# New tables for the order of work in a CIN and top-MLP kernel

## The chip, the cores and the metric

The kernel runs on one core of one Trainium2 chip. The metric is the device time of one execution in microseconds, as the median of the runs shown; lower is better.

## The reference, cut to what matters

Everything is float32. 512 samples each have 32 categorical fields; every field has a table of 16-wide rows. Three interaction layers and a small MLP follow:

```python
e = jnp.stack([tbl_f[ids[:, f]] for f in range(32)], axis=1)        # (512, 32, 16)
x0 = xk = e
for W in (W0, W1, W2):             # (32, 32, 64), (32, 64, 64), (32, 64, 64)
    xk = relu(jnp.einsum('bmd,bhd,mhk->bkd', x0, xk, W))             # (512, 64, 16)
    outs.append(jnp.sum(xk, axis=2))                                 # (512, 64)
h = jnp.concatenate([*outs, dense_ctx], axis=1)                      # (512, 208)
h = jnp.maximum(h @ W_top1 + b_top1, 0)                              # 512 wide
h = jnp.maximum(h @ W_top2 + b_top2, 0)                              # 256 wide
y = h @ W_top3                                                       # (512, 1)
```

## The kernel before

**Tiles and blocks.** The batch is cut into 8 pairs of 64 samples; a sample has 16 columns, so a pair has 1024. The first two pairs are cut in half again, which gives ten blocks (`BLOCKS`): blocks 0 to 3 are narrow (512 columns), 4 to 9 wide (1024). A *step* (layer, block) is one interaction layer of one block. Steps of layers 1 and 2 multiply 16 tiles of 128 rows (eight tiles of four fields, by two halves `g` of 32 of the 64 hidden rows) elementwise by a factor, and contract each product with weights on TensorE into 64 output rows. A layer-0 step has four tiles and a quarter-size one, the "opposite" product, because it uses the symmetry of the two equal operands.

**Who does what.** GpSimd gathers the table rows, one indirect DMA of 128 rows for each of 128 gathers (16 for a pair, 8 for a narrow block), with `gather` at L692 to L721. SyncE's queue copies a block's rows to DRAM (`scratch`) and loads them back, repeated over partitions, as `own`, `opposite` and `rotated` (`layer0_operands`, for layer 0) and as eight field tiles (`field_tiles`, for layers 1 and 2), in the order of `LOADS`. SyncE's queue is in order: a load that waits holds all that stand behind it. VectorE makes most products (L805, and L840, L845 in the narrow layer-0 steps) into a ring `vz` of nine tiles; GpSimd makes the rest (L746 into the four-tile ring `pz`; L729 for the opposite product into `oz`). `POOL_TILES` says how many of a step's 16 tiles GpSimd makes. TensorE contracts them (L1060), ScalarE takes the relu (L934), VectorE sums over the 16 columns of a sample (L855). The narrow blocks' layer-0 factors come from the gathered rows by matmuls ("turns", L998).

**The factor of layers 1 and 2** is the relu's output, each row repeated four times. Three ways lead to it. For a step in no table, ScalarE sends DMAs from the relu's output to `hidden` (the relay, L945) and copies `hidden` into PSUM (L890). For a step in `SPREAD`, TensorE writes both halves into PSUM by matmuls with a 0/1 matrix (L984), with no relay, and ScalarE copies one half to `hidden` (L904) if GpSimd has tiles of that step. For a step in `HALF`, TensorE writes the first half alone and the second goes by relay.

**Paired steps.** In a narrow step each weight meets 512 columns, usually in two matmuls of 256, one for each half of the output. For a step in `PAIRED` one matmul of 512 columns takes a tile, even tiles into the lower 64 rows and odd ones into the upper (L1055). At its end ScalarE copies the accumulator (`fold`, L917), TensorE adds the two halves with a 0/1 matrix (`join`, L1082), and the relu waits for that. The join stands in TensorE's order one item behind the step's last product.

**The order.** Nothing is decided at run time. `BEGUN` lists the 30 steps; VectorE's, TensorE's, GpSimd's and ScalarE's programs are derived from it (`vector_program`, `tensor_program`, `POOLS`, `scalar_program`), and each engine runs its own in order, with semaphores between them. `tensor_program` puts a spread behind the product that `spread_after` gives: soon after its source step has ended, or once the factor's place (a ring of three) is free. A step's products on TensorE stand as VectorE's and GpSimd's interleaved. `FIRST_GATHERS` gathers go ahead of GpSimd's first product; `GATHERS_IN` says how many go directly ahead of each product of a step. `PACED` lets gather `i` wait until TensorE has used so many of VectorE's products; `BEHIND_SPREAD` lets it wait for so many spreads. Block b's scratch waits for all its gathers (L586, L596 in `scratch`).

## Time and profile before

| what | value |
|---|---|
| runs shown | 338.79, 339.94, 414.93 us |
| median | 339.94 us |
| span of the profiled execution | 356.2 us |
| TensorE matmul busy | 314.8 us (88%) |
| VectorE busy | 282.1 us (79%) |
| GpSimd busy | 246.0 us (69%) |
| ScalarE busy | 53.3 us (15%) |

The page gives no other time of the profiled execution than its span, from its first to its last instruction. Busy times don't count DMA issues, semaphores or branches. The ends of matmuls are modelled, so back-to-back matmuls are better read from the chain of waits, which goes from start to start. All engines' times are microseconds from the start of the span, and a gather on GpSimd is a row of L719.

### The profile page before, as it was taken

The page shows a single profiled execution, that of the slowest core. Times are in us where ns is not written, and L with a number is a line of the kernel's source. Part 1 is how long each engine was busy: PE and PEld are TensorE (multiplying, and loading weights), DVE is VectorE, ACT ScalarE, POOL GpSimd, SP SyncE. Part 2 cuts the span into 40 slices and gives each one's busy share as a digit, 9 for nine tenths or more (in the row PEclk, how much of TensorE's full clock was granted, in tenths as well). Part 3 has the DMA queues.
Part 4 walks back from the last instruction along what each step waited for, and adds up shares of the span by engine and source line. Part 5 has one row for each costly group of instructions (what it writes and reads, how often), then busy time and mean ns, then how long its engine had stood idle before and what let it go on. Part 6 is the DMA issues. An engine that isn't in the chain of part 4 may idle for free.

```text
span 356.2 us, 4290 instructions
## 1 busy us (share of the span) xinstructions
PE 314.8 (88%) x1602; PEld 114.9 (32%) x1602; DVE 282.1 (79%) x172; ACT 53.3 (15%) x77; POOL 246.0 (69%) x195
## 2 busy tenths in 40 slices
PE   0378588988699788898999999998999999999997
PEld 0344224432222223332333333332333333333334
DVE  0039477869499878999999999999998879999220
ACT  1000011012020221110112120121022111220011
POOL 5646566766367668869997987896998569729300
PEclk9999989999899999999999999999999999999999
DMA  6272853834875982979499989683699897050000
GB/s 183 65 231 72 230 154 73 230 71 110 295 240 174 326 292 65 326 217 280 167 317 289 296 284 297 201 268 67 215 346 337 290 291 194 17 133 2 0 0 0
DMA packets 34302, 68.09 MB, mean 191 GB/s; under 512 B 5866, under 2 KB 15082, under 8 KB 34282
## 3 DMA queue, kind: packets, MB, share of 16 engines
q1 hardware_dynamic: 23562, 56.80, 49.0%
q10 hardware_dynamic: 6624, 9.96, 9.4%
q0 software_dynamic: 4096, 1.06, 3.5%
q8 instruction: 12, 0.20, 0.2%
q14 instruction: 8, 0.07, 0.1%
HBM read 55.55 MB, written 2.03 MB: 162 GB/s over the span
## 4 chain that ended last, share of the span: by engine, by line
PE 59%; POOL 16%; issue 11%; DVE 9%; another core or an unknown queue 2%; DMA 1%; DVEq 1%; ACT 0%; POOLq 0%; SPq 0%
PE acc L1060 37%; PE acc L1055 12%; POOL gathered L719 10%; DVE vz L805 8%; POOL pz L746 6%; PE factor L984 2%; PE factor L1093 2%; PE factor L1021 1%; PE factor L1088 1%; PE acc L1050 1%; PE factor L998 1%; PE acc L1082 1%; PE factor L1100 1%; DVEq L800 1%
## 5 line engine op out<-in xcount | busy, mean ns | idle before, releaser
L805 DVE TENSOR_TENSOR vz<-fields_sb,factor 128x1024 f32<-128x1024 f32 (+3 forms) x113 | 230.5, 2090 | 20.7 <-PE factor L984 7.6
L1060 PE MATMUL acc<-vz,w_sb 128*64 128x512 f32 (+1 forms) x800 | 172.6, 569 | 10.9 <-DVE vz L805 3.6
L719 POOL DMA_INDIRECT gathered<-in_table,index x128 | 121.6, 950 | 65.0 <-issue 31.5
L746 POOL TENSOR_TENSOR pz<-fields_sb,hidden 128x1024 f32<-128x1024 f32 (+1 forms) x52 | 117.9, 2292 | 19.4 <-DMA hidden<-relu_out 9.6
L1060 PEld LDWEIGHTS acc<-vz,w_sb 128*64 128x64 f32 x800 | 57.8, 139 | 113.7 <-issue 98.6
L1055 PE MATMUL acc<-vz,w_sb 128*64 128x512 f32 x216 | 60.9, 621 | 3.7 <-DVE vz L805 2.9
L1060 PE MATMUL acc<-pz,w_sb 128*64 128x512 f32 x192 | 48.1, 594 | 0.3 <-POOL pz L746 0.3
L934 ACT ACTIVATE relu_out<-acc 128x512 f32<-128x512 f32 (+1 forms) x30 | 15.3, 512 | 126.3 <-PE acc L1060 47.3
L890 ACT ACTIVATE factor<-hidden 128x1024 f32<-128x1024 f32 (+1 forms) x23 | 20.1, 878 | 65.8 <-DMA hidden<-relu_out 34.3
L805 DVE TENSOR_TENSOR vz<-rotated,factor 128x2048 f32<-128x2048 f32 x12 | 26.9, 2279 | 1.8 <-issue 1.8
L1055 PEld LDWEIGHTS acc<-vz,w_sb 128*64 128x64 f32 x216 | 16.4, 139 | 36.4 <-issue 24.6
L855 DVE TENSOR_REDUCE feats<-relu_out 128x32 f32<-128x512 f32 (+1 forms) x30 | 17.1, 571 | 7.9 <-ACT relu_out L934 7.7
L1060 PEld LDWEIGHTS acc<-pz,w_sb 128*64 128x64 f32 x192 | 13.5, 137 | 28.1 <-issue 23.9
L1021 PE MATMUL factor<-gathered,unit_sb 32*128 32x128 f32 x8 | 1.6, 493 | 15.0 <-DMA gathered<-in_table,index 15.0
L984 PE MATMUL factor<-relu_out,unit_sb 32*128 32x512 f32 (+1 forms) x68 | 11.4, 553 | 3.8 <-issue 3.3
L917 ACT ACTIVATE folds<-acc 128x512 f32<-128x512 f32 x7 | 4.2, 597 | 47.5 <-PE acc L1055 43.4
L845 DVE TENSOR_TENSOR vz<-own,factor 128x1024 f32<-128x1024 f32 x4 | 4.7, 1217 | 6.4 <-remote 4.1
L1050 PE MATMUL acc<-oz,w0c_sb 128*64 128x256 f32 (+1 forms) x72 | 8.3, 349 | 1.3 <-POOL oz L729 1.3
L822 DVE TENSOR_TENSOR vz<-own,factor 128x512 f32<-128x512 f32 x2 | 1.4, 688 | 9.8 <-ACT own L896 9.3
L890 ACT ACTIVATE factor<-own 128x1024 f32<-128x1024 f32 x6 | 6.2, 1026 | 13.0 <-POOL pz L746 13.0
L984 PEld LDWEIGHTS factor<-relu_out,unit_sb 32*128 32x128 f32 x68 | 3.9, 190 | 12.7 <-issue 11.8
L774 DVE TENSOR_TENSOR w_sb<-vz 128x256 f32<-128x256 f32 x1 | 0.4, 425 | 8.5 <-DMA w0c_sb<-in_w0c 8.5
(44 smaller groups left out, 83.2 us busy)
## 6 DMA issues: line engine op xcount, KB each, us to landing
fields_sb<-fields SPq DMA_DIRECT2D x48, 512.0 KB
rotated<-fields SPq DMA_DIRECT2D x24, 512.0 KB
fields_sb<-fields SPq DMA_DIRECT2D x32, 256.0 KB
hidden<-relu_out ACTq DMA_DIRECT2D x30, 256.0 KB, 5.6
own<-fields SPq DMA_DIRECT2D x6, 512.0 KB
gathered<-in_table,index POOLq DMA_INDIRECT x128
hidden<-relu_out ACTq DMA_DIRECT2D x16, 128.0 KB
fields<-gathered SPq DMA_DIRECT2D x6, 256.0 KB, 5.2
```

Of the source, the lines that this page charges most:

```text
L719: nc.gpsimd.indirect_dma_start(gathered[:, pair % GRING, j, :], None, table, bass.IndirectOffsetOnAxis(ap=index[:, i:i + 1], axis=0)).then ...
L746: nc.gpsimd.tensor_tensor(pz[:, at % PRING, 0:cols], fields[s][:, t, col:col + cols], hidden_of(step, g), ALU.mult).then_inc(pz_ready, 1)
L805: nc.vector.tensor_tensor(vz[:, at:at + nt, 0:cols].rearrange("p t (a n) -> p t a n", n=half), src[:, t:t + nt, col:col + cols].rearrange( ...
L855: nc.vector.tensor_reduce(feats[layer][:, pair, first:first + count], relu_of(step).rearrange("p (b d) -> p b d", d=DIM), op=ALU.add, axis ...
L890: nc.scalar.activation(factor_of(step, g), src.rearrange("p (a n) -> p a n", a=2), ACT.Copy).then_inc(factor_put, 1)
L934: nc.scalar.activation(relu_of(step), acc[:, n % 2, 0:half], ACT.Relu).then_inc(relu_done, 1)
L984: last = nc.tensor.matmul(factor_of(step, g)[:, ab, :], unit_sb[row:row + HROWS, :], relu_of(before)[row:row + HROWS, :], start=True, stop ...
L1021: last = nc.tensor.matmul(slot_of(step, held)[:, ab, wave * quarter:(wave + 1) * quarter], by, rows[row, :], start=True, stop=True)
L1050: last = nc.tensor.matmul(acc_of(step, q // 2)[:, part], w0c_sb[:, by_field(b), q, :], quarters, start=False, stop=q % 2 == 1)
L1055: last = nc.tensor.matmul(acc[side % 2 * HID:(side % 2 + 1) * HID, ORDER.index(step) % 2, 0:cols], w_sb[layer][:, kt, :], z, start=side < ...
L1060: last = nc.tensor.matmul(acc_of(step, ab), w_sb[layer][:, kt, :], z[:, ab * half:(ab + 1) * half], start=start and j == 0, stop=stop and ...
L1093: return nc.tensor.matmul(to, wt2_sb[:, k, m * P:(m + 1) * P], rows, start=k == 0, stop=k == F_TOP1 // P - 1)
```

## The change

Only tables at the head of the file are set anew; no function changes.

- `BEGUN`: (1,3) goes ahead of (2,2); (2,3) ahead of (0,5), which then stands between (2,3) and (1,4); (0,6) ahead of (2,4); (2,6) ahead of (0,8).
- `SPREAD` and `HALF`: (1,4) and (1,5) turn from whole spreads to halves; (2,2) and (1,3) from halves to whole ones; (2,4), (1,7) (halves) and (1,9) (whole) leave the tables and go by relay.
- `POOL_TILES`: GpSimd's tiles in the narrow steps go from 4 to 7, in the wide ones from 48 to 46.
- `FIRST_GATHERS`, `GATHERS_IN`, `PACED`, `BEHIND_SPREAD`: 23 gathers ahead of the first product for 21; the rows of gathers between products are cut otherwise (the longest 21 for 24), the waits are other ones, and many of them ask for fewer products.
- `PAIRED`: (1,2) alone is left of seven.
- `LOADS`: block 1's field tiles go behind block 2's operands; block 3's field tiles ahead of block 4's scratch and operands.

```diff
-BEGUN = [(0, 0), (1, 0), (0, 1), (2, 0), (0, 2), (1, 1), (0, 3), (1, 2), (2, 1), (2, 2), (1, 3), (0, 4), (0, 5),
-    (2, 3), (1, 4), (1, 5), (2, 4), (0, 6), (2, 5), (0, 7), (1, 6), (1, 7), (0, 8), (2, 6), (2, 7), (0, 9), (1,
-    8), (1, 9), (2, 8), (2, 9)]
+BEGUN = [(0, 0), (1, 0), (0, 1), (2, 0), (0, 2), (1, 1), (0, 3), (1, 2), (2, 1), (1, 3), (2, 2), (0, 4), (2,
+    3), (0, 5), (1, 4), (1, 5), (0, 6), (2, 4), (2, 5), (0, 7), (1, 6), (1, 7), (2, 6), (0, 8), (2, 7), (0,
+    9), (1, 8), (1, 9), (2, 8), (2, 9)]
...
-SPREAD = [(1, 0), (2, 3), (1, 4), (1, 5), (1, 9)]
-HALF = [(2, 0), (1, 2), (2, 2), (1, 3), (2, 4), (1, 7), (2, 7)]
-POOL_TILES = {(1, 0): 0, (2, 0): 0, (1, 1): 1, (2, 1): 0, (1, 2): 0, (2, 2): 0, (1, 3): 0, (2, 3): 3, (1, 4): 1,
-    (1, 5): 5, (2, 4): 3, (2, 5): 4, (1, 6): 4, (1, 7): 3, (2, 6): 4, (2, 7): 5, (1, 8): 6, (1, 9): 4, (2, 8): 3,
-    (2, 9): 6}
-FIRST_GATHERS = 21
-GATHERS_IN = {(0, 1): (2,), (0, 2): (11,), (1, 1): (1,), (0, 3): (7,), (0, 4): (24,), (0, 5): (15,), (2, 3): (2,
-    0, 1), (1, 4): (2,), (1, 5): (10, 0, 0, 2, 0), (2, 4): (3, 0, 0), (0, 6): (2,), (2, 5): (7, 0, 0, 0), (1, 6):
-    (0, 1, 0, 2), (1, 7): (3, 4, 0), (0, 8): (8,)}
-PACED = {12: 1, 13: 2, 14: 4, 17: 5, 18: 6, 19: 7, 20: 8, 22: 9, 24: 11, 25: 14, 26: 15, 28: 16, 29: 17, 30: 18,
...
-    74, 97: 78, 99: 80, 102: 83, 104: 84, 106: 85, 107: 86, 109: 87, 112: 96, 114: 97, 117: 99, 119: 100, 121:
-    102, 122: 103, 125: 104, 126: 105, 127: 106}
-BEHIND_SPREAD = {10: 1, 11: 3, 15: 4, 24: 5, 26: 6, 36: 7, 43: 8, 45: 9, 55: 10, 61: 11, 80: 12, 85: 13, 93: 14}
+SPREAD = [(1, 0), (1, 3), (2, 2), (2, 3)]
+HALF = [(2, 0), (1, 2), (1, 4), (1, 5), (2, 7)]
+POOL_TILES = {(1, 0): 0, (2, 0): 0, (1, 1): 2, (2, 1): 1, (1, 2): 1, (2, 2): 0, (1, 3): 0, (2, 3): 3, (1, 4):
+    0, (1, 5): 4, (2, 4): 3, (2, 5): 4, (1, 6): 4, (1, 7): 3, (2, 6): 5, (2, 7): 5, (1, 8): 5, (1, 9): 4, (2,
+    8): 5, (2, 9): 4}
+FIRST_GATHERS = 23
+GATHERS_IN = {(0, 2): (10,), (1, 1): (1, 3), (1, 2): (3,), (2, 1): (10,), (0, 4): (3,), (2, 3): (21, 2, 2),
+    (0, 5): (5,), (1, 5): (8, 4, 0, 2), (2, 4): (0, 3, 1), (2, 5): (1, 9, 0, 0), (1, 6): (1, 0, 2, 0), (1, 7):
+    (6, 2, 1), (2, 6): (2, 0, 0, 1, 1), (0, 8): (1,)}
+PACED = {12: 1, 13: 2, 14: 3, 15: 4, 16: 4, 18: 4, 20: 7, 21: 8, 22: 10, 24: 11, 25: 13, 26: 14, 27: 15, 28:
...
+    78, 103: 78, 104: 79, 105: 79, 106: 80, 109: 81, 111: 88, 112: 92, 114: 93, 115: 93, 116: 93, 117: 93,
+    119: 94, 122: 98, 126: 101, 127: 102}
+BEHIND_SPREAD = {10: 1, 24: 5, 36: 7, 45: 9, 48: 9, 50: 9, 61: 11, 80: 12, 84: 12, 85: 13, 91: 13, 100: 14,
+    104: 14, 105: 14, 107: 14, 117: 14, 122: 14}
...
-PAIRED = [(2, 0), (1, 1), (1, 2), (2, 1), (2, 2), (1, 3), (2, 3)]
+PAIRED = [(1, 2)]
...
-LOADS = [('scratch', 0), ('fields', 0), ('scratch', 1), ('operands', 1), ('fields', 1), ('scratch', 2),
-    ('operands', 2), ('scratch', 3), ('operands', 3), ('fields', 2), ('scratch', 4), ('operands', 4), ('fields',
-    3), ('scratch', 5), ('operands', 5), ('fields', 4), ('fields', 5), ('scratch', 6), ('operands', 6),
+LOADS = [('scratch', 0), ('fields', 0), ('scratch', 1), ('operands', 1), ('scratch', 2), ('operands', 2),
+    ('fields', 1), ('scratch', 3), ('operands', 3), ('fields', 2), ('fields', 3), ('scratch', 4), ('operands',
+    4), ('scratch', 5), ('operands', 5), ('fields', 4), ('fields', 5), ('scratch', 6), ('operands', 6),
...
```

The rest of `LOADS` is the same in both: scratch and operands of a block, then field tiles, up to `('scratch', 9), ('operands', 9), ('fields', 8), ('fields', 9)`.

## Rows read from the trace of the kernel before

**Rows 1.** The page's head.

```profile
span 356.2 us, 4290 instructions
```

**Rows 2.** Busy time by stretch: engines' busy us (instructions), granted clock, DMA share, GB/s.

```profile
75.00:100.00 25.00, 20.69 (x99) 7.22 (x99) 20.14 (x19) 4.06 (x8) 15.09 (x16) 0.93 0.64 192
250.00:300.00 50.00, 50.00 (x242) 16.82 (x240) 45.84 (x22) 8.02 (x10) 42.12 (x20) 1.00 0.87 283
```

**Rows 3.** VectorE in order of time: start, us, what [idle before <- its releaser].

```profile
41.56 2.48 DVE L840 TENSOR_TENSOR vz<-own,factor 128x512 f32<-128x512 f32 x4 [3.47 <-remote]
97.43 1.75 DVE L805 TENSOR_TENSOR vz<-fields_sb,factor 128x1536 f32<-128x1536 f32 x1 [4.86 <-PE acc L1055]
126.94 2.29 DVE L805 TENSOR_TENSOR vz<-rotated,factor 128x2048 f32<-128x2048 f32 x1 [1.84 <-issue]
141.79 3.35 DVE L805 TENSOR_TENSOR vz<-fields_sb,factor 128x3072 f32<-128x3072 f32 x1 [1.26 <-issue]
277.44 3.35 DVE L805 TENSOR_TENSOR vz<-fields_sb,factor 128x3072 f32<-128x3072 f32 x1 [2.33 <-PE acc L1060]
291.47 6.62 DVE L805 TENSOR_TENSOR vz<-fields_sb,factor 128x3072 f32<-128x3072 f32 x2 [1.83 <-issue]
```

**Rows 4.** TensorE in order of time, the spread for (2,2).

```profile
92.46 0.70 PE L984 MATMUL factor<-relu_out,unit_sb 32*128 32x256 f32 x4 [3.29 <-issue]
```

**Rows 5.** The chain of waits in order of time: start, us, what.

```profile
60.17 1.08 PE acc L1060 x8
...
76.44 1.73 PE acc L1060 x16
...
88.74 0.43 PE acc L1082 x4
...
165.45 1.06 PE factor L984 x4
...
290.28 1.07 PE factor L984 x8
291.35 46.50 PE acc L1060 x216
```

**Rows 6.** ScalarE in order of time: three relus, and copies of a factor.

```profile
92.02 0.38 ACT L934 ACTIVATE relu_out<-acc 128x256 f32<-128x256 f32 x1 [3.62 <-issue]
...
103.52 0.38 ACT L934 ACTIVATE relu_out<-acc 128x256 f32<-128x256 f32 x1 [0.36 <-PE acc L1082]
...
125.55 0.38 ACT L934 ACTIVATE relu_out<-acc 128x256 f32<-128x256 f32 x1 [2.83 <-PE acc L1082]
125.83 1.02 ACT L890 ACTIVATE factor<-own 128x1024 f32<-128x1024 f32 x1
...
239.47 1.03 ACT L890 ACTIVATE factor<-hidden 128x1024 f32<-128x1024 f32 x1 [3.81 <-DMA hidden<-relu_out]
```

**Rows 7.** Groups by shape: count, busy us, mean ns of one, idle time before them.

```profile
L746 POOL TENSOR_TENSOR pz<-fields_sb,hidden 128x1024 f32<-128x1024 f32 x48 | 112.8, 2375 | 19.3 <-DMA hidden<-relu_out 9.6 <-PE acc L1060 5.1 <-DMA fields_sb<-fields 2.0
L805 DVE TENSOR_TENSOR vz<-fields_sb,factor 128x3072 f32<-128x3072 f32 x30 | 99.6, 3345 | 5.4 <-issue 3.1 <-PE acc L1060 2.3
L805 DVE TENSOR_TENSOR vz<-fields_sb,factor 128x1024 f32<-128x1024 f32 x43 | 49.9, 1212 | 8.7 <-PE factor L984 7.6 <-remote 1.1
L805 DVE TENSOR_TENSOR vz<-fields_sb,factor 128x1536 f32<-128x1536 f32 x14 | 24.3, 1748 | 6.6 <-PE acc L1055 6.3 <-PE acc L1060 0.3
```

**Rows 8.** GpSimd in order of time, from (1,5)'s fourth product to gather 127.

```profile
168.82 4.72 POOL L746 TENSOR_TENSOR pz<-fields_sb,hidden 128x1024 f32<-128x1024 f32 x2
...
174.98 0.94 POOL L719 DMA_INDIRECT gathered<-in_table,index  x1 [0.30 <-issue]
...
247.10 0.94 POOL L719 DMA_INDIRECT gathered<-in_table,index  x1 [1.70 <-PE acc L1060]
248.06 0.73 POOL L729 TENSOR_TENSOR oz<-gathered,opposite 128x256 f32<-128x256 f32 x1
```

**Rows 9.** SyncE's queue: the field tiles of blocks 8 and 9.

```profile
258.19 29.40 SPq L653 DMA_DIRECT2D fields_sb<-fields  x16
```

More of the change, by code:

```diff
@@ L118 @@
 IN_FLIGHT_DIRECT = 3
-LOADS = [('scratch', 0), ('fields', 0), ('scratch', 1), ('operands', 1), ('fields', 1), ('scratch', 2),
-    ('operands', 2), ('scratch', 3), ('operands', 3), ('fields', 2), ('scratch', 4), ('operands', 4), ('fields',
-    3), ('scratch', 5), ('operands', 5), ('fields', 4), ('fields', 5), ('scratch', 6), ('operands', 6),
-    ('scratch', 7), ('operands', 7), ('fields', 6), ('fields', 7), ('scratch', 8), ('operands', 8), ('scratch',
-    9), ('operands', 9), ('fields', 8), ('fields', 9)]
+LOADS = [('scratch', 0), ('fields', 0), ('scratch', 1), ('operands', 1), ('scratch', 2), ('operands', 2),
+    ('fields', 1), ('scratch', 3), ('operands', 3), ('fields', 2), ('fields', 3), ('scratch', 4), ('operands',
+    4), ('scratch', 5), ('operands', 5), ('fields', 4), ('fields', 5), ('scratch', 6), ('operands', 6),
+    ('scratch', 7), ('operands', 7), ('fields', 6), ('fields', 7), ('scratch', 8), ('operands', 8),
+    ('scratch', 9), ('operands', 9), ('fields', 8), ('fields', 9)]
 OWN, ACROSS = -1, L0TILES
```

7 rows, old and new, of the table PACED are left out of this document.

## The prediction

> **What bounds the kernel now.** I read the page's span, then busy time by stretch, the idle time in front of VectorE's products, the chain of waits, and the queues of ScalarE, GpSimd and SyncE. The profiled execution's span is 356.2 us [rows 1]; the page gives no other time for it. The median of the three runs shown is 339.94 us, 16.3 us less than this span, so the profiled execution was slow. I work the sum in its microseconds, take it off the median too, and say which stalls may belong to the profiled execution alone.
>
> There are two regimes. From 250 to 300 us TensorE is busy 50.00 of 50 us; from 75 to 100 it is busy 20.69 of 25 and VectorE 20.14 [rows 2]. Late, VectorE waits for TensorE: 2.33 us at 277.4 (no free slot in `vz`) and 1.83 us at 291.5 [rows 3]. In the chain the last stage of it is 216 matmuls in 46.50 us with no gap, 215 ns each, and behind them come the top layers [rows 5]. So late the end moves with TensorE's work. Early it moves with VectorE's stalls, because TensorE is fed by it.
>
> **The change part by part**, by step (layer, block).
>
> (a) *Block 5's layer 0 goes behind (2,3).* Its second product, at 126.94, came after 1.84 us of idling [rows 3]. The profile shows why in ScalarE's queue: the relu of (1,3) ran at 125.55, having waited 2.83 us for the join of that paired step, and block 5's factor copy stood behind it [rows 6]. After the change (1,3) has no join, and 13 tiles of (2,3) lie ahead of (0,5). I take -1.84. The step (1,4) started after 1.26 us of waiting for its spread at 141.79 [rows 3]; now (0,5), two products of 2.3 us, stands between, long enough to cover that: -1.26. What is late next is the matmul queue itself.
>
> (b) *One join for seven.* A join costs TensorE 0.43 us [rows 5]; six go, 2.6 us, all before 150 us, where TensorE is not the limit. I count them at nothing; TensorE's idle quarter to eighth there is the cover, and if it is gone the gain is 2.6. The unpaired step issues 64 matmuls of 256 columns for 32 of 512. Sixteen of 256 took 1.73 us, 108 ns each [rows 5], half of 215, so the width costs nothing by this row. The bigger stall is at 92.46: TensorE stood 3.29 us in front of the spread for (2,2), which waited for the relu of the paired (1,2) [rows 4], and VectorE then lost 4.86 us at 97.43 for want of a slot [rows 3]. In the new order that spread stands behind (1,3)'s fourth product, far from the relu. The gain lies between 0 and 4.86. That relu came 3.62 us after ScalarE's previous work, while the relu of the next paired step idled 0.36 us [rows 6], with the same code. I therefore hold most of this stall for the profiled execution's own and take -0.5, nearest to the ordinary join.
>
> (c) *Loads.* Block 1's field tiles now follow block 2's operands on SyncE's queue, so block 1's `own` copy flies alone. VectorE waited 3.47 us for (0,1) at 41.56 [rows 3], released by something the profile cannot name. Bounds: -3.47, or a little above 0 if the later tiles hold (1,1). I take 0, since (2,0) behind it needs the relu of (1,0) in any case. Block 3's tiles go ahead of block 4's operands, which (1,3)'s earlier place needs; block 4's step is not due until some 30 us later, which hides it.
>
> (d) *GpSimd tiles.* VectorE gives three narrow tiles away, 1748 - 1212 = 536 ns each, 1.6 us, and takes back two wide ones, 3345 / 3 = 1115 ns each, 2.2 us [rows 7]. Net +0.6, with ends -1.6 (the wide ones hidden in VectorE's 4.2 us of late waiting for TensorE) and +2.2. The early products stand ahead of gathers on GpSimd; the gathers' weaker waits pay for them.
>
> (e) *Other spreads.* A spread of a wide step holds TensorE 1.06 us as a half (four matmuls) and 1.07 as a whole (eight) [rows 5], so turning (1,4) and (1,5) into halves gives nothing; three wide ones disappear, those of (2,4), (1,7) and (1,9): 3 x 1.07 = -3.2 us in TensorE's saturated stretch. In their place ScalarE sends DMAs and copies 1.03 us per factor [rows 6], with 10 us or more of other steps as cover; if that is gone, up to 3.2 is given back. The narrow ones only change kind.
>
> (f) *(2,6) ahead of (0,8), and where the gathers stand.* (2,6) now starts where (0,8) did, at about 239.4, but its factor is copied from 239.47 to 240.50 [rows 6]: +1.1. The last gather, 127, now stands behind all five products of (2,6). From the start of (1,5)'s fourth product GpSimd had 30 gathers and 16 large products up to the end of gather 127, 168.82 to 248.04, 79.2 us [rows 8]; now it has 31 gathers and 20 large products from there: 31 x 1.25 + 20 x 2.375 [rows 7] + 2 small ones x 0.74 = 87.7 (1.25 from the 0.95 of a gather and the 0.30 in front of it [rows 8]). It comes 8.5 us later if GpSimd is as late there as now. Behind it on SyncE are block 9's scratch, its operands, and then the field tiles of block 8, from 258.19, 29.40 us for 16 [rows 9]: 1.84 us each, so the eighth is in by about 258.2 + 8 x 1.84 + 3 x 1.84 = 278.4 (an estimate, three in flight). (1,8)'s second product needs it at 277.44 + 3.35 + 0.5 = 281.3 [rows 3]. So 2.9 of the 8.5 are slack and VectorE may wait 5.6. The cover is VectorE's 2.33 + 1.83 us of waiting for TensorE, and that GpSimd comes earlier, since its gathers' waits for matmuls loosen (1.70 us in front of gather 127 alone [rows 8]). I take 0 for the tiles, with 5.6 as the other end.
>
> Sum: -1.84 - 1.26 - 0.5 + 0.6 - 3.2 + 1.1 = -5.1 us. That makes 351.1 of the profiled 356.2, and **334.8** of the median 339.94.
>
> A rule speaks against (b). The Trainium skill's page "TensorE: Matmul & The Clock Gate", section "Back-to-back issue gap", says that in a stream of weight loads and matmuls the spacing is set by both, 81 ns at 128 columns and 131 ns at 512. Read between these, two matmuls of 256 would take about 196 ns against 131 (an estimate from that page), and 192 such pairs 12.5 us more, which would turn the sum into +7.4. The 108 ns against 215 of this kernel's rows disagree with it.
>
> **The rivals.** A measurement of this kernel can tell about 2%, 6.8 us: faster is below 333.1, slower above 346.7.
>
> 1. *The early stalls belong to every run.* Then the 4.86 us at 97.43 go whole: 334.8 - 4.4 = 330.4, and 327.8 if the six joins also counted. For it: the stall hangs on an order in which a spread stands straight behind a join, and that order goes. Against it: the relu's lateness has no cause in the rows, and the median is 16.3 us under the span.
>
> 2. *GpSimd's last gather becomes the path.* Block 9's rows come late, block 8's tiles behind them on SyncE's queue later still, and (1,8) waits. Early gains are then waited out, since GpSimd's own chain sets the time: 339.94 + 5.6 + 1.1 - 1.07 (the spread behind it) = 345.6, slower than before. It decides from the point where gather 127 is issued over 2.9 us later than 247.1, counted against (1,7)'s end. For it: the count of 87.7 against 79.2. Against it: VectorE's 4.2 us of slack and the looser waits.
>
> 3. *The gain doesn't reach the end.* The three engines are so evenly loaded late that without the spreads TensorE waits for VectorE, which has 2.2 us more to do there, and (a)'s stalls turn up in front of (1,4) in another form: 339.94 - 3.2 + 2.2 = 338.9.
>
> 4. *Narrow matmuls are dearer.* Eight of 256 columns alone span 1.08 us in the chain [rows 5], 135 ns each with their drain. At that price 384 cost 51.8 us against 192 x 0.215 = 41.3: +10.5 on TensorE early, and with no cover 334.8 + 10.5 = 345.3. The row of 16 speaks against it, and only pieces of the stretch could pay it. The page named above is what would favour it.
>
> **How the numbers follow.** Chances: forecast 0.45, rival 1 0.22, rival 2 0.17, rival 3 0.11, rival 4 0.05. The forecast's own range is 331 to 338.5. The whole range reaches down to 328 (rival 1 with the joins) and up to 343, which takes in rival 3 and the lower part of rivals 2 and 4. Faster by over 2%: a third of the forecast and nearly all of rival 1, 0.37. Slower by over 2%: a third of rival 2 and of rival 4, 0.08. Within 2%: 0.55.
>
> **What would show it.** In the changed profile the products of (0,5) and (1,4) should start with no wait; no spread should follow a join with TensorE standing; TensorE should have no gap from about 165 us on, with one wide spread left there beside that of (1,5). VectorE should wait for TensorE, not for field tiles, in front of (1,8). If it waits there for tiles, and gather 127 was issued later than some 10 us behind the end of (1,7)'s products, rival 2 is right. If TensorE shows holes behind GpSimd's products of (2,5) or (2,6), part (f) was priced too low. If the early stretch still loses 3 to 4 us at a time with no order behind it, those stalls are not the tables' doing.

## The result and the profile after

The changed kernel takes **360.17 us** (median of 5 runs, 359.79 to 364.84) against 339.73 of the kernel before, run beside it: a ratio of 1.064, 95% interval [1.061, 1.068]. It is slower by 20.4 us, where 334.8 was forecast and the range ended at 343. Medians here and below are over all runs, while ratios are worked out from the single runs without the disturbed ones (414.93 us of the kernel before, one run each of e4 and e13), so that a ratio is not the quotient of two medians.

The page of the changed kernel, its head, its first part and its chain of waits by engine, and below that the chain of the kernel before, from its second profile (run e5 below):

```profile
span 363.0 us, 4599 instructions
## 1 busy us (share of the span) xinstructions
PE 311.2 (86%) x1754; PEld 124.5 (34%) x1754; DVE 283.0 (78%) x171; ACT 51.8 (14%) x72; POOL 245.9 (68%) x196
...
PE 40%; DMA 26%; DVE 15%; issue 9%; POOL 6%; SPq 2%; ACT 1%; ACTq 0%; DVEq 0%; POOLq 0%
```

```profile
PE 78%; DVE 12%; issue 5%; POOL 2%; DMA 1%; DVEq 0%; ACT 0%; SPq 0%
```

No engine has over 1 us more to do than in the table of the time before. What has grown is the waiting: DMA is 26% of the chain that ended last, for 1%.

Both profiled spans must first be put side by side with care. The kernel before was profiled once more (run e5 below): 339.09 us with a span of 337.3, not 356.2 [rows 1]. This clean profile is what the changed kernel is held against from here on. The changed kernel's own profiled execution took 364.84 us, 4.7 above its median: its rows show where it waits and for what, and the price of a wait is read from the runs further down. Its file is two lines longer, so that a gather is a row of L721. Busy time by stretch of the changed kernel (columns as in [rows 2]), then of the clean kernel before:

```profile
75.00:100.00 25.00, 24.30 (x170) 11.62 (x170) 25.00 (x25) 1.97 (x4) 18.19 (x19) 0.93 0.59 184
150.00:200.00 50.00, 40.63 (x184) 13.39 (x186) 47.22 (x22) 10.39 (x12) 40.54 (x31) 0.99 0.83 268
275.00:300.00 25.00, 17.60 (x72) 5.70 (x70) 16.30 (x7) 3.27 (x5) 12.31 (x6) 0.86 0.93 309
```

```profile
75.00:100.00 25.00, 24.24 (x108) 7.73 (x106) 24.44 (x23) 4.89 (x9) 18.00 (x20) 1.00 0.73 228
150.00:200.00 50.00, 50.00 (x244) 17.14 (x240) 49.86 (x23) 10.19 (x12) 44.12 (x30) 1.00 0.85 277
250.00:300.00 50.00, 50.00 (x242) 16.80 (x240) 47.31 (x22) 8.98 (x11) 32.68 (x16) 1.00 0.71 219
```

In the clean kernel before, TensorE is busy 50.00 of 50 us from 150 to 200 and VectorE 49.86: both are full. After the change TensorE has holes there (40.63 of 50) and a large one from 275 to 300.

The holes are named by the idle time in front of TensorE's matmuls. TensorE of the changed kernel in order of time (start, us, what [idle before <- releaser]):

```profile
118.62 0.65 PE L1062 MATMUL acc<-pz,w_sb 128*64 128x256 f32 x4 [1.51 <-POOL pz L748]
122.31 0.65 PE L1062 MATMUL acc<-pz,w_sb 128*64 128x256 f32 x4 [2.17 <-POOL pz L748]
...
190.93 2.77 PE L1062 MATMUL acc<-vz,w_sb 128*64 128x512 f32 x12
198.64 1.61 PE L1062 MATMUL acc<-pz,w_sb 128*64 128x512 f32 x4 [4.93 <-POOL pz L748]
...
281.40 4.26 PE L1062 MATMUL acc<-vz,w_sb 128*64 128x512 f32 x12 [2.85 <-DVE vz L807]
...
291.06 4.49 PE L1062 MATMUL acc<-vz,w_sb 128*64 128x512 f32 x12 [4.55 <-DVE vz L807]
```

The three with a `pz` wait for GpSimd's products of (2,3) and (2,5), the last two for VectorE in (1,8). VectorE there, in order of time:

```profile
277.90 3.35 DVE L807 TENSOR_TENSOR vz<-fields_sb,factor 128x3072 f32<-128x3072 f32 x1 [3.70 <-DMA fields_sb<-fields]
...
287.65 3.35 DVE L807 TENSOR_TENSOR vz<-fields_sb,factor 128x3072 f32<-128x3072 f32 x1 [5.81 <-ACT factor L892]
...
302.71 3.35 DVE L807 TENSOR_TENSOR vz<-fields_sb,factor 128x3072 f32<-128x3072 f32 x1 [2.38 <-DMA fields_sb<-fields]
```

The same place in the clean kernel before, the first products of (1,8) and (1,9):

```profile
258.55 3.35 DVE L805 TENSOR_TENSOR vz<-fields_sb,factor 128x3072 f32<-128x3072 f32 x1 [0.86 <-PE acc L1060]
...
272.57 6.62 DVE L805 TENSOR_TENSOR vz<-fields_sb,factor 128x3072 f32<-128x3072 f32 x2 [1.83 <-issue]
```

These answer to the last two of [rows 3]: where VectorE waited 0.86 us for TensorE it now waits 3.70 for a field tile. The 5.81 are put down to a factor copy, but (1,8)'s own two copies had run at 270.16 and 274.08, and the one that ended at 287.60 is (1,9)'s. What that product still needed was a field tile: it multiplies tiles 3 to 5, and GpSimd's third product of (1,8), which takes tile 5 alone, waited for its tile up to 287.60 too (below). So all three are waits for tiles. GpSimd of the changed kernel in order of time, and then SyncE's queue, show where the tiles were:

```profile
62.63 0.46 POOL L731 TENSOR_TENSOR oz<-gathered,opposite 128x128 f32<-128x128 f32 x1 [4.91 <-DMA opposite<-fields]
...
70.01 1.27 POOL L748 TENSOR_TENSOR pz<-fields_sb,hidden 128x512 f32<-128x512 f32 x1 [3.29 <-DMA fields_sb<-fields]
...
195.24 0.95 POOL L721 DMA_INDIRECT gathered<-in_table,index  x1 [0.30 <-issue]
196.21 6.98 POOL L748 TENSOR_TENSOR pz<-fields_sb,hidden 128x1024 f32<-128x1024 f32 x3
...
252.62 0.98 POOL L721 DMA_INDIRECT gathered<-in_table,index  x1 [0.16 <-issue]
...
280.09 2.35 POOL L748 TENSOR_TENSOR pz<-fields_sb,hidden 128x1024 f32<-128x1024 f32 x1 [12.98 <-DMA fields_sb<-fields]
...
287.60 7.00 POOL L748 TENSOR_TENSOR pz<-fields_sb,hidden 128x1024 f32<-128x1024 f32 x3 [2.16 <-DMA fields_sb<-fields]
```

```profile
45.80 8.85 SPq L655 DMA_DIRECT2D fields_sb<-fields  x8
...
106.23 0.38 SPq L593 DMA_DIRECT2D fields<-gathered  x1
...
254.95 0.38 SPq L593 DMA_DIRECT2D fields<-gathered  x1
...
264.08 33.25 SPq L655 DMA_DIRECT2D fields_sb<-fields  x16
```

The last gather, 127, is issued at 252.62; block 9's scratch follows at 254.95 and the field tiles of blocks 8 and 9 from 264.08, in 33.25 us for 16 where [rows 9] had 29.40 from 258.19. GpSimd itself idles 12.98 us for such a tile. The three products at 196.21 are those of (2,5) that TensorE waited for at 198.64; nine gathers stood ahead of them. In the clean kernel before gather 127 was issued at 228.19, 24.4 us sooner. Part of that is its place and part a lag of everything in front: VectorE's last product of (1,7) ended at 222.0 there and at 237.5 here, so that behind that product gather 127 came after 6.2 us and comes after 15.1, 8.9 us more.

GpSimd of the clean kernel before, in the stretch where this lag begins, and its SyncE queue:

```profile
63.73 0.47 POOL L729 TENSOR_TENSOR oz<-gathered,opposite 128x128 f32<-128x128 f32 x1
...
66.90 0.94 POOL L719 DMA_INDIRECT gathered<-in_table,index  x1 [0.30 <-issue]
68.14 0.94 POOL L719 DMA_INDIRECT gathered<-in_table,index  x1 [0.30 <-issue]
...
130.15 0.94 POOL L719 DMA_INDIRECT gathered<-in_table,index  x1 [0.30 <-issue]
131.40 0.94 POOL L719 DMA_INDIRECT gathered<-in_table,index  x1 [0.30 <-PE acc L1060]
```

```profile
32.59 9.73 SPq L653 DMA_DIRECT2D fields_sb<-fields  x8
...
96.02 0.38 SPq L591 DMA_DIRECT2D fields<-gathered  x1
```

A gather is busy for 0.94 us and the next one starts 1.25 us after it, with 0.30 us "issue" between. From gather 43 at 65.65 to gather 80 at 114.12 there are 37 in 48.5 us, 1.31 us each with one opposite product among them, and waits beyond the 0.30 come to under 2 us in all: GpSimd has practically no slack in this stretch, although the windows count it busy 18.00 of 25 us. What is put in front of these gathers, a product or a wait, can be made up only out of those 2 us. Here block 1's field tiles were issued from 32.59, ahead of the loads of blocks 2 and 3; in the changed kernel they were issued from 45.80, ahead of block 3's loads and block 2's tiles, and the two waits of GpSimd at 62.63 and 70.01 are for block 3's `opposite` and a tile of block 2. VectorE of the changed kernel waits for tiles of blocks 1 and 2 as well, in (1,1) and (1,2):

```profile
58.28 2.35 DVE L807 TENSOR_TENSOR vz<-fields_sb,factor 128x1024 f32<-128x1024 f32 x2 [2.86 <-DMA fields_sb<-fields]
...
73.81 2.35 DVE L807 TENSOR_TENSOR vz<-fields_sb,factor 128x1024 f32<-128x1024 f32 x2 [2.93 <-DMA fields_sb<-fields]
```

In the changed kernel gather 47 was issued 9.6 us later than in the clean one (80.22 for 70.64), gather 63 12.0 later (103.81 for 91.83), and block 5's scratch, which waits for gather 63, 10.2 later (106.23 for 96.02).

### The profile page after: what moved, and what is told of

Read it like the earlier page. It is cut to its first block, busy times and chain, and to the rows that moved or that the text cites. A ratio compares the mean times of both kernels' runs of the same rounds, so it can differ in the third digit from the quotient of the medians.

```text
span 363.0 us, 4599 instructions
## 1 busy us (share of the span) xinstructions
PE 311.2 (86%) x1754; PEld 124.5 (34%) x1754; DVE 283.0 (78%) x171; ACT 51.8 (14%) x72; POOL 245.9 (68%) x196
## 4 chain that ended last, share of the span: by engine, by line
PE 40%; DMA 26%; DVE 15%; issue 9%; POOL 6%; SPq 2%; ACT 1%; ACTq 0%; DVEq 0%; POOLq 0%
PE acc L1062 33%; DVE vz L807 14%; DMA fields_sb<-fields 12%; DMA fields<-gathered 5%; POOL gathered L721 4%; DMA hidden<-relu_out 4%; DMA rotated<-fields 4%; PE acc L1057 2%; POOL pz L748 2%; PE factor L1095 2%; DMA gathered<-in_table,index 1%; PE factor L1090 1%; SPq L655 1%; PE acc L1052 1%; PE factor L1102 1%
## 5 line engine op out<-in xcount | busy, mean ns | idle before, releaser
L1062 PE MATMUL acc<-vz,w_sb 128*64 128x512 f32 (+1 forms) x1168 | 225.3, 521 | 18.8 <-DVE vz L807 17.1
L721 POOL DMA_INDIRECT gathered<-in_table,index x128 | 122.3, 955 | 39.6 <-issue 27.1
L1062 PEld LDWEIGHTS acc<-vz,w_sb 128*64 128x64 f32 x1168 | 83.3, 140 | 145.8 <-issue 93.2
L1062 PE MATMUL acc<-pz,w_sb 128*64 128x512 f32 (+1 forms) x208 | 51.2, 582 | 12.3 <-POOL pz L748 12.2
L892 ACT ACTIVATE factor<-hidden 128x1024 f32<-128x1024 f32 (+1 forms) x27 | 25.2, 932 | 95.8 <-DVE vz L807 44.6
L1062 PEld LDWEIGHTS acc<-pz,w_sb 128*64 128x64 f32 x208 | 14.7, 138 | 42.6 <-issue 22.0
L1057 PE MATMUL acc<-vz,w_sb 128*64 128x512 f32 x30 | 9.3, 714 | 2.1 <-DVE vz L807 2.0
L731 POOL TENSOR_TENSOR oz<-gathered,opposite 128x256 f32<-128x256 f32 (+1 forms) x9 | 5.8, 645 | 6.7 <-DMA opposite<-fields 6.7
L986 PE MATMUL factor<-relu_out,unit_sb 32*128 32x256 f32 (+1 forms) x52 | 7.6, 476 | 0.5 <-ACT relu_out L936 0.5
L1052 PEld LDWEIGHTS acc<-oz,w0c_sb 128*64 128x64 f32 x72 | 4.8, 137 | 5.9 <-issue 2.9
L871 DVE TENSOR_SCALAR vz<-factor,bt_sb 128x512 f32<-128x512 f32 x2 | 1.5, 751 | 6.6 <-PE factor L1102 6.6
## 6 DMA issues: line engine op xcount, KB each, us to landing
hidden<-relu_out ACTq DMA_DIRECT2D x12, 128.0 KB, 4.2
```

The costliest lines, as they stand in the source:

```text
L721: nc.gpsimd.indirect_dma_start(gathered[:, pair % GRING, j, :], None, table, bass.IndirectOffsetOnAxis(ap=index[:, i:i + 1], axis=0)).then ...
L731: nc.gpsimd.tensor_tensor(oz[:, 0:quarter], quarter_rows(step[1]), opposite[s][:, at:at + quarter], ALU.mult).then_inc(pz_ready, 1)
L892: nc.scalar.activation(factor_of(step, g), src.rearrange("p (a n) -> p a n", a=2), ACT.Copy).then_inc(factor_put, 1)
L986: last = nc.tensor.matmul(factor_of(step, g)[:, ab, :], unit_sb[row:row + HROWS, :], relu_of(before)[row:row + HROWS, :], start=True, stop ...
L1052: last = nc.tensor.matmul(acc_of(step, q // 2)[:, part], w0c_sb[:, by_field(b), q, :], quarters, start=False, stop=q % 2 == 1)
L1057: last = nc.tensor.matmul(acc[side % 2 * HID:(side % 2 + 1) * HID, ORDER.index(step) % 2, 0:cols], w_sb[layer][:, kt, :], z, start=side < ...
```

## The experiments

Theory **G** is that GpSimd's order is the cause: rows of gathers ahead of products that TensorE needs, and products and waits ahead of gathers that the loads need. Rival **P** is that the stalls seen before belong to the profiled execution; **L1** that SyncE's new order of loads costs by itself; **N** (the prediction's rival 4) that narrow matmuls are dearer. Differences below are between medians; where two kernels ran on different chips, the ratio to the kernel before is given beside.

**e1 to e4: the rows of gathers of the changed kernel, cut otherwise.**

```
e1:  (2, 6): (2, 0, 0, 1, 1), (0, 8): (1,)   ->  (2, 6): (5, 0, 0, 0, 0)
e2:  (2, 5): (1, 9, 0, 0)                    ->  (2, 5): (10, 0, 0, 0)
e3:  (2, 3): (21, 2, 2), (0, 5): (5,)        ->  (2, 3): (17, 0, 0), (0, 5): (13,)
e4:  all three
```

> The changed kernel with gathers 123 to 127 all ahead of (2,6)'s first GpSimd product, nothing else. Theory G (gather rows stand in the wrong places): block 9's rows come some 12 us sooner, block 8's field tiles start when (2,6) is done, the waits in front of (1,8) (3.70, 5.81 and 2.38 us on VectorE, 2.85 and 4.55 on TensorE) go, and the time falls by 5 to 8 us, to 352 to 355. Rival L (load order and narrow matmuls make the loss early, and the late waits are only where it surfaces): the waits move elsewhere and the time stays within 2 us of 360.2.

> The changed kernel with the nine gathers ahead of (2,5)'s second GpSimd product moved ahead of its first. Theory G: TensorE's wait of 4.93 us for that product at 198.6, and the half clock behind it, mostly go, while the first product comes some 2 us late: 3 to 6 us less, 354 to 357. Rival L: within 2 us of 360.2, because the wait for block 8's tiles further on sets the time whatever happens here.

> The changed kernel with 17 gathers ahead of (2,3)'s first GpSimd product instead of 21 and none between its three products; the eight go ahead of (0,5)'s. Theory G: TensorE's three waits for these products (1.51, 2.17, 1.12 us) go and block 3's end comes 4 us sooner; 2 to 5 us less, 355 to 358. Rival L: within 2 us of 360.2.

> The three edits of the gather rows together. Theory G: the sum of them less what overlaps, 10 to 17 us less, 343 to 350, with the rest of the loss left for load order or narrow matmuls. Rival L: under 6 us less.

e1: 353.63 us, 6.5 less than 360.17 (ratio to the kernel before 1.042 [1.038, 1.046]), as theory G has it; gather 127 is issued at 237.25, and of VectorE's waits for tiles in (1,8) and (1,9) none is left, while the one in front of (2,7) grew from 1.64 to 3.80. e2 and e3 gained nothing: 362.73 (1.065 [1.060, 1.070]) and 362.34 (1.067 [1.062, 1.071]); both expectations missed. Together (e4) they gave 348.98 (1.026 [1.023, 1.030]), 11.2 less. So e2's and e3's cuts are worth nothing while gather 127 stays where it was (253.24 and 250.34 in them): (1,8) waits the gain out again (3.52 and 5.10 us in e2, 3.52 and 5.49 in e3), as the prediction's rival 2 has it. With gather 127 in its new place they are worth 4.65 (e4 against e1). In e3 the wait for (2,3)'s products turned into one for the opposite product of (0,5). In e4 it is still there; TensorE in order of time:

```profile
130.36 1.97 PE L1052 MATMUL acc<-oz,w0c_sb 128*64 128x256 f32 x8 [5.94 <-POOL oz L731]
```

**e5: the kernel before, profiled again.**

> The kernel before, unchanged, profiled once more. Theory P (the profiled execution of before was slow by itself): span near 338 us, and the stalls of 4.86 us at 97.4 and 3.47 us at 41.6 on VectorE are gone or under 1 us, so that the step (1,5) ends some 15 us sooner than at 171.8. Rival: span near 356 again with the same stalls, which then belong to the tables.

339.09 us, span 337.3. The stalls of 4.86 us at 97.43 and of 3.29 on TensorE at 92.46 [rows 3, 4] are gone, as is the 1.26 in front of (1,4); the 3.47 at 41.56 is 1.17. The one in front of (0,5) is there (1.75 us); it is the first of that step's two products, not the second as the prediction has it. P holds: most of the early stalls of the first profile were that execution's own, as the prediction guessed.

**e6: other rows once more, for the whole kernel.** Against e4, the gathers of (0,5) go into (1,5), and those of (2,4) to (2,6) are cut otherwise.

```
(1, 5): (25, 4, 0, 0), (2, 4): (0, 2, 1), (2, 5): (4, 0, 0, 0), (1, 6): (2, 2, 2, 0), (1, 7): (6, 2, 2), (2, 6): (6, 0, 0, 0, 0)
```

> The mended gather rows of the last run, and besides no gathers ahead of (0,5)'s product (they go to (1,5), where GpSimd waits for field tiles), and those of (2,5) spread further on. Theory G: TensorE's wait of 5.9 us for that product and VectorE's 3.1 us in (2,5) go, 3 to 6 us less than 349.0: 343 to 346, within 2% of before. Rival L: what is left of the loss is early, in load order or narrow matmuls, and the time stays at 347 to 350.

A miss: 352.70 (1.037 [1.031, 1.043]), 3.7 more than e4. The waits moved, to 4.8 us in front of (2,7) and 2.1 in (0,6). A row of gathers can't be placed by hand for one waiting product at a time.

**e7 and e8, from e6: the loads, and the pairing.**

```
e7:  LOADS: ('operands', 1), ('fields', 1), ('scratch', 2), ...     (block 1's field tiles as before)
e8:  PAIRED = the seven steps of the kernel before
```

> As e6, with block 1's field tiles behind block 1's operands again, as before. Theory L1 (late tiles of block 1 hold (1,1), and push block 2's tiles and (1,2) back): VectorE's waits for field tiles at 56 and 71 us (1.6 and 3.4) go, 2 to 5 us less than e6. Rival: own copy of block 1 then flies beside them, (0,1) waits instead, and nothing is gained.

> As e6, with all seven narrow steps paired again. Theory G says that unpairing cost nothing: within 2 us of e6, or up to 3 us slower, since six joins and folds come back. Rival N (narrow matmuls are dearer than their row showed, or the added instructions have to be fetched): 4 to 10 us faster than e6.

e7: 348.25 (1.024 [1.019, 1.029]), 4.45 less than e6, as L1 has it. VectorE's waits for tiles in (1,1) and (1,2) are gone (2.72 and 3.94 us in e6), and GpSimd's two (5.25 and 2.92 in e6) are nothing and 0.44; gather 47 comes at 74.31 for 80.98. Which of the two engines' waits carries the 4.45 isn't told apart. e8: 351.40 (1.036 [1.032, 1.040]), not told apart from e6. N fails: with the tables of this order the unpaired steps cost nothing that could be measured.

**e9, from e7: the early GpSimd products back as before.**

```
POOL_TILES (1, 1): 2 -> 1, (2, 1): 1 -> 0, (1, 2): 1 -> 0, with the gathers around them cut as (1, 1): (1,), (0, 3): (6,), (0, 4): (13,)
```

> The kernel of e7 with the early GpSimd products as before: (1,1) gives 1 tile to GpSimd, (1,2) and (2,1) none, and gathers 24 to 63 are cut as before around them. Theory E: an early GpSimd product that waits for a field tile or a relay holds the gathers of pairs 2 and 3 that stand behind it in GpSimd's order; so gather 63 comes some 7 us sooner than at 100 us in e7, block 4's field tiles and block 6's operands are loaded sooner, the waits in (1,4) (4.7 us together) and (0,6) (3.6) go in part, and the time is 3 to 6 us below e7's 348.25: 342 to 345. Rival: gather 63 is set by its own waits and the loads ahead of it in SyncE's queue; VectorE only takes three narrow tiles more (3 x 0.54 = 1.6 us), and the time is 347 to 350.

345.99 (1.019 [1.016, 1.022]), 2.3 less than e7, between theory and rival, and the intervals overlap. Gather 63 came 2.7 us sooner (96.37 for 99.09), not 7. VectorE makes one product more in (1,1) than in e7, and the waits of `PACED` count its products and were left as they were, so that behind it each asks for one product fewer: part of the 2.3 may be that.

**e10 to e12, and e14 to e16: one part of the change alone, in the kernel before.**

```
e10: PAIRED = [(1, 2)]
e11: (2, 4), (1, 7) out of HALF, (1, 9) out of SPREAD
e12: POOL_TILES (1, 1): 2, (2, 1): 1, (1, 2): 1; gathers (1, 1): (1, 0), (0, 3): (7,), (1, 2): (3,), (2, 1): (10,), (0, 4): (11,)
e14: block 1's field tiles behind block 2's operands
e15: (2, 3) ahead of (0, 5); gathers (2, 3): (12, 0, 1), (0, 5): (5,)
e16: (2, 6) ahead of (0, 8); gathers (2, 6): (8, 0, 0, 0)
```

> The kernel before with one change alone: of seven paired steps only (1,2) stays paired. The prediction's term (b): six joins of 0.43 us go where TensorE is not the limit; time unchanged to 2.6 us less (337 to 339.7, against 339.7). Rival 4 (narrow matmuls are dearer): up to 10.5 us more, 342 to 350.

> The kernel before with one change alone: the spreads of (2,4), (1,7) and (1,9) are gone, their factors go by relay. The prediction's term (e): 3 x 1.07 us of TensorE less in its saturated stretch, 336.5. Rival: the relays come late or VectorE is as full as TensorE there, and the time is 339 to 343.

> The kernel before with one change alone: GpSimd makes one narrow tile more in each of (1,1), (2,1) and (1,2), as in the changed kernel, with the gathers around them cut to stand the same. Theory E: these products wait for field tiles or relays with gathers behind them; gather 63 comes some 5 to 8 us later than at 92.8, SyncE's queue moves with it, and the time is 3 to 7 us above 339.7. Rival (the prediction's term (d)): the gathers' waits pay for them, VectorE saves 1.6 us, and the time is 338 to 340.

> The kernel before with one change alone: block 1's field tiles behind block 2's operands in SyncE's queue. The prediction's term (c): 0 (336.3 to 340). Theory L1, from e7: block 1's and 2's tiles come late for (1,1) and (2,1), 2 to 5 us more: 341.5 to 344.5.

> The kernel before with one change alone: (2,3) ahead of (0,5), with 12 gathers ahead of (2,3)'s first GpSimd product, one ahead of its third and 5 ahead of (0,5)'s. The prediction's term (a): -1.84 and -1.26, 336.6. Theory O: the paired (1,3)'s relu then stands directly ahead of (2,3), which needs it, so the wait only moves and grows: 340 to 346.

> The kernel before with one change alone: (2,6) ahead of (0,8), with the 8 last gathers ahead of (2,6)'s first GpSimd product, so that gather 127 stands where it did. The prediction's term (f) without the late gather: +1.1, 340.8. Theory O: GpSimd's first product of (2,6), behind the 8 gathers, is late for TensorE by the 4 us that a (0,8) took: 343 to 347.

| run | part | us | ratio to before | against 339.3 to 339.5 |
|---|---|---|---|---|
| e10 | (b) one pairing for seven | 335.86 | 0.990 [0.987, 0.993] | -3.5 |
| e11 | (e) three wide spreads gone | 341.76 | 1.008 [1.005, 1.011] | +2.4 |
| e12 | (d) early GpSimd products | 365.96 | 1.078 [1.074, 1.082] | +26.6 |
| e14 | (c) block 1's field tiles later | 340.55 | 1.003 [1.001, 1.005] | +1.1 |
| e15 | (a) (0,5) behind (2,3) | 338.49 | 0.998 [0.995, 1.001] | -1.0 |
| e16 | (f) (2,6) ahead of (0,8) | 346.26 | 1.018 [1.013, 1.023] | +6.8 |

The interval of e15 takes in 1, and that of e14 begins just above it. e10 is the one part that gains clearly, and more than expected; it is also a version that **beats both kernels**, by 1.0% (clear of its interval, but under the 2% that the prediction asks of a faster kernel) and, over the two ratios, by 7.0%. Its source is read in two places. VectorE in order of time: the first product of (0,5) in the clean kernel before, and the two products of (0,4) and this one in e10, now with no wait:

```profile
111.53 2.29 DVE L805 TENSOR_TENSOR vz<-rotated,factor 128x2048 f32<-128x2048 f32 x1 [1.75 <-ACT factor L890]
```

```profile
103.97 6.67 DVE L805 TENSOR_TENSOR vz<-rotated,factor 128x2048 f32<-128x2048 f32 x3
```

ScalarE's relu of (1,3) in the same two, which answers to the third relu of [rows 6]:

```profile
110.14 0.38 ACT L934 ACTIVATE relu_out<-acc 128x256 f32<-128x256 f32 x1 [2.85 <-PE acc L1082]
```

```profile
105.24 0.38 ACT L934 ACTIVATE relu_out<-acc 128x256 f32<-128x256 f32 x1 [8.00 <-PE acc L1060]
```

In the kernel before (1,3)'s relu ran at 110.14, 4.7 us after VectorE's last product of that step; without the join it runs at 105.24, 1.1 us after it, and block 5's factor copy behind it in ScalarE's queue is no longer late. VectorE is 1.3 us ahead at the end of (1,3) (104.1 for 105.4), 3.1 at the end of (0,5) (113.2 for 116.3), and 3.2 at its last product (309.5 for 312.7).

In e11 VectorE's steps up to (2,7) end within 0.2 us of where they did (222.1 for 222.0 at (1,7), 253.4 for 253.3 at (2,7)): TensorE's two spreads less changed nothing for it. TensorE has holes instead: from 200 to 250 us it is busy 48.52 of 50, VectorE 50.00. Then VectorE waits in (1,8) and (1,9). VectorE of e11 in order of time:

```profile
259.35 3.35 DVE L805 TENSOR_TENSOR vz<-fields_sb,factor 128x3072 f32<-128x3072 f32 x1 [1.56 <-PE acc L1060]
...
277.74 3.35 DVE L805 TENSOR_TENSOR vz<-fields_sb,factor 128x3072 f32<-128x3072 f32 x1 [1.16 <-DMA fields_sb<-fields]
```

The clean kernel before has 0.86 at the first of these and nothing at the second. That the relays in the spreads' place are the cause isn't shown: e14, with its spreads as before, waits 0.77 us for the same tile.

e15 moves (0,5) behind (2,3), and the wait moves to the first products of (2,3), in front of their spread:

```profile
111.13 2.35 DVE L804 TENSOR_TENSOR vz<-fields_sb,factor 128x1024 f32<-128x1024 f32 x2 [1.64 <-PE factor L983]
```

e16 shows what the place between two large steps was for. TensorE, VectorE and GpSimd of e16 in order of time:

```profile
231.82 1.97 PE L1060 MATMUL acc<-pz,w_sb 128*64 128x512 f32 x4 [3.65 <-POOL pz L746]
```

```profile
238.24 2.29 DVE L805 TENSOR_TENSOR vz<-fields_sb,factor 128x2048 f32<-128x2048 f32 x1 [4.76 <-PE acc L1060]
```

```profile
228.44 0.94 POOL L719 DMA_INDIRECT gathered<-in_table,index  x1 [1.54 <-PE acc L1060]
229.40 9.28 POOL L746 TENSOR_TENSOR pz<-fields_sb,hidden 128x1024 f32<-128x1024 f32 x4
```

The last gathers end at 229.4 and GpSimd's first product of (2,6) comes out at 231.8; with (0,8) in front TensorE had that time to spend, with (2,6) in front it stands.

**e13 and e17: what of e12's 26.6 us is the products' own.** e13 is e12 with the waits of gathers 24 to 63 as in the changed kernel; e17 is e12 with the gathers cut as there:

```
e17: GATHERS_IN (1, 1): (0, 3), (1, 2): (3,), (2, 1): (10,), (0, 4): (16,), none in (0, 3)
```

> The kernel of e12 (the kernel before with one early GpSimd product more in each of (1,1), (2,1) and (1,2)), and the waits of gathers 24 to 63 as in the changed kernel, which ask for fewer products and fewer spreads. If the early products cost what they do because of the strong waits around them, the weak ones give back most of e12's 26.6 us: 339 to 346. If the products themselves hold the queue, whatever the waits: 355 to 366.

> The kernel of e12 (the kernel before with three narrow tiles more for GpSimd in (1,1), (1,2) and (2,1)) with its gathers cut as in the changed kernel: 37, 40 and 50 gathers stand ahead of the second product of (1,1) and those of (1,2) and (2,1), for 35, 45 and 55 in e12. If e12's 26.6 us come from the place of (2,1)'s product behind five gathers more (TensorE waited 3.4 us for it at 84.5), most of them go: 340 to 346. If an early product holds the gathers wherever it stands: 355 to 366.

e13: 361.89 (1.065 [1.061, 1.069]); e17: 360.56 (1.059 [1.054, 1.064]). The weaker waits of e13 give back 4.1 of the 26.6 us, the other place 5.4: neither is all of it. e17 is the cleaner trace. GpSimd in order of time:

```profile
65.51 1.27 POOL L746 TENSOR_TENSOR pz<-fields_sb,hidden 128x512 f32<-128x512 f32 x1 [2.85 <-DMA fields_sb<-fields]
...
137.48 0.94 POOL L719 DMA_INDIRECT gathered<-in_table,index  x1 [1.87 <-PE acc L1060]
141.35 0.94 POOL L719 DMA_INDIRECT gathered<-in_table,index  x1 [2.92 <-PE acc L1060]
```

Two products (1.28 us and 0.16 behind each, 2.9 us) and a wait of 2.85 put gather 47 5.1 us behind the clean kernel before (75.70 for 70.64). The third product stands behind gather 49 and adds 1.4. Gather 63 is 5.0 us behind (96.86), gather 80 5.2 (119.33): over 33 gathers about as much is caught up as the third product costs, and no more. VectorE meanwhile gained from the tiles given away (it ended (2,2) at 94.2 for 96.0) and lost it in (1,3), which waits for block 3's tiles and ends at 107.3 for 105.4. Up to the end of (2,3) the loss is 3.7 us (128.0 for 124.3).

The remaining 17 us of e17 come later, and here these three experiments have a **flaw**: VectorE makes one product fewer in (1,1) (the second half's seven tiles go as 3, 2 and 2, its six as 3 and 3), and the waits that count its products were left as they were, so that from there on each asks for one product more. Gathers 87 and 88 wait 1.87 and 2.92 us where the clean kernel before had 0.30 each. How much of the 21 to 27 us is this and how much the products' own lag isn't told apart; the nearest size for the changed kernel is e9's 2.3, where the same count shifts the other way.

**e18, from e9: (0,8) ahead of (2,6) again,** with the last six gathers ahead of (0,8)'s product.

> The kernel of e9 with (0,8) ahead of (2,6) again, as in the kernel before, and the last six gathers ahead of (0,8)'s product. Theory O, from e16 (that order costs the kernel before 6.8 us): 4 to 6.8 us below e9's 345.99, 339 to 342. Rival: e9's rows of gathers are made for its order, and the time stays at 345 to 348.

343.90 (1.016 [1.011, 1.021]), 2.1 less than e9, where 4 to 6.8 were expected; the intervals overlap. The trace shows the order's part: VectorE ends (2,7) at 256.3 for 261.7, and gives 2.6 us back in front of (1,8).

## Why the prediction was wrong

**The account.** From 360.17: the rows of gathers 11.2 (e4), the loads 4.45 (e7), the early products 2.3 (e9), less 3.7 that e6's rows lost. That reaches 345.99, and (2,6)'s place takes off 2.1 more (343.9). Each of these was measured on top of those before it, and e9's and e18's intervals overlap with their neighbours'. What is left, 4.5 us to the kernel before (339.38 beside e18) and 8.0 to the unpaired one of e10, stays open: by e11 the missing spreads can be 2.4 of it, and in e9 (0,6), which now stands ahead of (2,4), waits 1.77 and 0.92 us for block 6's `rotated`. Neither was tried by itself in that kernel, and neither were the waits of `PACED` and `BEHIND_SPREAD`, (1,3)'s earlier place or the shifted tiles of the wide steps.

**Step (f) failed**, and with it the sum. It put gather 127 behind all products of (2,6), worked out that VectorE might then wait 5.6 us for block 8's tiles, and took 0, because gathers' "waits for matmuls loosen". The count was good: 8.5 us later, and measured from the end of (1,7) gather 127 came 8.9 later. The zero was not: the gathers in front came later and not sooner, and e1, which moved the last five forward, gained 6.5. The mechanism and the size of that wait stood in the text as rival 2, at a chance of 0.17, and so did its sign, a gather 127 over 10 us behind (1,7) (15.1) with (1,8) waiting for tiles. Its time, 345.6, was still 14.6 short: it counted that wait alone, and neither the rows of gathers, the loads nor the early products. The cover that the step named was smaller than read: VectorE's late waiting for TensorE, 2.33 and 1.83 us in the first profile [rows 3], is 0.86 and 1.83 in the clean one. Nothing in the prediction priced the rows of gathers in front of (2,3) and (2,5), where TensorE waited 1.51, 2.17 and 4.93 us for GpSimd; with e1's cut they are worth 4.65 (e4). The step's other half, +1.1 for (2,6)'s early start, was 6.8 in e16, with eight gathers in front of it, and 2.1 in e18: only the factor copy was counted, not GpSimd's products behind their gathers.

**Step (d) failed in its last sentence**, "the gathers' weaker waits pay for them". The gathers from 65 to 114 us of the clean kernel before wait for hardly anything that a table could weaken; most follow each other at 1.25 us. [rows 8] had that figure and the sum used it, but only for the end of the kernel. Weaker waits gave back 4.1 us of 26.6 in e13. For the changed kernel itself the early products' price is known no better than as e9's 2.3 us, where the step had +0.6 in all. **(c)**, taken at 0, cost 4.45 us in the changed order and 1.1 in the kernel before. The bound that it named, later tiles that hold (1,1), came true (2.86 us at 58.28), and with it (1,2) (2.93 at 73.81) and two waits of GpSimd in front of gathers (4.91 and 3.29 us at 62.63 and 70.01). In the kernel before the opposite product that waited 4.91 stands five gathers further back, which is a likely reason for the smaller cost there.

**Step (e) failed in sign**: -3.2 forecast, +2.4 measured (e11). TensorE's 50.00 of 50 us [rows 2] were read as "the end moves with TensorE's work"; VectorE is as full there (49.86 of 50 from 150 to 200 in the clean profile, 50.00 of 50 from 200 to 250), so that TensorE's relief there bought nothing. Rival 3 had said this. Where the added 2.4 come from is open but for the two waits that e11's rows show.

**Step (b) was right in what it rejected and too small in its size.** The narrow matmuls cost nothing (e8, e10). The Trainium skill's page "TensorE: Matmul & The Clock Gate", section "Back-to-back issue gap", weighed there against the row, would have made unpairing 12.5 us dearer by the estimate. The trace does not agree: TensorE was busy 304.8 us in e10 for 309.2 in the clean kernel before, and e10 measured 3.5 us less, so the row decides. The gain was put at -0.5, with a reason that held (the 4.86 us were the execution's own), but the same joins also delayed block 5's factor, which the prediction booked under (a). That is why **(a)** measured -1.0 for -3.1 (e15), not told apart from nothing: moving (0,5) hands the wait to (2,3), which waits 1.64 us in its place, and leaving out the join removes it; the 1.26 in front of (1,4) was the first profile's own.

**The base was a disturbed execution**, and the prediction said so; it even named the right stalls. What it did not do is ask what the late stages look like without them: of VectorE's 4.2 us of slack on which (f) and (d) leaned, 2.7 are left in the clean rows. Rival 1, which built on those stalls, was at 0.22 against rival 2's 0.17.

## What to carry to other kernels

Before work is put in front of an in-order queue, read that queue's start-to-start spacing: here an engine that issued DMAs back to back counted as busy 18.00 of 25 us and had hardly any slack, and a lag of 5.1 us was still 5.2 us 33 gathers later (e17). In a closed loop of gathers, loads, products and waits an early lag can come back as late tiles elsewhere, so that one mended wait alone often shows nothing (e2, e3); mend the one that ends last first. A profile that is 5% above the median of the runs is to be used for durations, not for slack.

## What the runs showed of the hardware

The same program's profiled execution spanned 356.2 us once and 337.3 us once, with nothing in the rows that gives the cause. TensorE's granted clock fell around its long holes: the mean was 0.86 of 2.4 GHz from 275 to 300 us of the changed kernel, where TensorE was busy 17.60 of 25 us, so part of that stretch ran at the 1.2 GHz level; right behind its idle times of 2.85 and 4.55 us, 12 matmuls took 4.26 and 4.49 us, against 2.77 for 12 at 190.93. Thus each of these two holes cost 1.5 to 1.7 us more than its length. A short one did not: behind the 1.04 us of idling at 187.47, 12 matmuls took 2.79.
